# First and fourth attention: second key tile spilled ahead of all stacking, loads requested behind the spills of queries and keys

## The reference, cut to what matters

```python
# x: (16, 112, 256), ctx: (16, 375, 256), 16 heads of 16
qh = heads(layernorm(x) @ W_q.T + b_q)      # layer 3: without biases
kh = heads(ctx @ W_k.T + b_k)
vh = heads(ctx @ W_v.T + b_v)
scores = einsum('bhqd,bhkd->bhqk', qh, kh) / sqrt(16)
attn = softmax(masked(scores), axis=-1)
out = einsum('bhqk,bhkd->bhqd', attn, vh) @ W_o.T (+ b_o)
x = x + out
```

## Time and profile before

| | us |
|---|---|
| median of 3 runs | 2326.16 |
| lowest and highest | 2322.23, 2326.8 |
| the profiled execution | 2323.39 |
| its span, first to last instruction | 2321.6 |
| first attention, about | 26 to 340 |
| fourth attention, about | 1893 to 2222 |

### The profile page before, as it was taken

The page is one execution under the profiler, slowest core; times in us unless marked ns, Lnnn a source line. Parts: engine busy times, 40 slices in busy tenths (PEclk is TensorE's granted clock), DMA queues, the critical chain, the costliest instruction groups (busy, mean ns, idle before and its releaser), DMA issues.

```text
span 2321.6 us, 46633 instructions
## 1 busy us (share of the span) xinstructions
PE 2169.4 (93%) x16038; PEld 1759.9 (76%) x16038; DVE 1285.7 (55%) x3563; ACT 1074.0 (46%) x2929; POOL 448.3 (19%) x478
## 2 busy tenths in 40 slices
PE   7999989999988899999999999999959979988998
PEld 6888877777666667678888788888747758877888
DVE  6877873222244522556556556555542238778766
ACT  5878872222223122244444444444402237877863
POOL 3112201111153345100000000000014421121150
PEclk9999999999999799999999999999969989999999
DMA  8677746222265322110000000001232257767701
GB/s 211 184 193 181 183 116 276 79 86 91 71 178 166 128 66 68 41 46 8 19 27 16 12 14 13 12 8 48 95 113 62 64 143 185 188 175 178 179 19 33
DMA packets 154867, 230.65 MB, mean 99 GB/s; under 512 B 66608, under 2 KB 127488, under 8 KB 152336
## 3 DMA queue, kind: packets, MB, share of 16 engines
q1 hardware_dynamic: 142160, 196.07, 30.4%
q0 software_dynamic: 10656, 29.37, 4.1%
q10 hardware_dynamic: 1824, 2.23, 0.4%
HBM read 176.36 MB, written 51.25 MB: 98 GB/s over the span
## 4 chain that ended last, share of the span: by engine, by line
PE 77%; DVE 7%; DMA 5%; issue 4%; SPq 3%; ACT 2%; POOL 1%; ACTq 0%; DVEq 0%; POOLq 0%
PE bank L2012 9%; PE bank L1157 8%; PE bank L2045 6%; PE bank L1188 6%; PE bank L1043 6%; PE bank L1039 6%; PE bank L2077 5%; PE bank L1083 4%; PE bank L1142 4%; PE bank L1028 3%; PE bank L1135 3%; PE bank L2062 3%; SPq L1523 2%; DMA query_halves<-arena 2%; PE bank L2398 2%
## 5 line engine op out<-in xcount | busy, mean ns | idle before, releaser
L1157 PE MATMUL bank<-ident,arena 112*125 112x112 f32 x2352 | 376.0, 278 | 2.2 <-DVE arena L1395 0.3
L1157 PEld LDWEIGHTS bank<-ident,arena 112*125 112x125 f32 x2352 | 342.8, 191 | 32.2 <-ACT arena L1428 5.8
L1428 ACT ACTIVATE arena<-arena,mx 112x375 f32<-112x375 f32 x512 | 309.3, 605 | 108.6 <-DVE mx L1374 104.5
L1374 DVE CUSTOM_DVE_ANT_0 arena<-bank,maskf 112x375 f32<-112x375 f32 x512 | 272.8, 541 | 101.3 <-PE bank L1135 96.8
L1428 ACT ACTIVATE arena<-bank,mx 112x375 f32<-112x375 f32 x272 | 154.8, 573 | 183.0 <-DVE mx L1386 155.4
L2012 PE MATMUL bank<-arena 128*128 x532 | 231.7, 558 | 2.1 <-ACT arena L2138 2.1
L1135 PE MATMUL bank<-kS,qS 128*112 128x376 f32 x512 | 204.9, 401 | 28.6 <-DMA qS<-query_halves 13.9
L1395 DVE COPY arena<-bank 125x336 f32<-125x336 f32 x448 | 214.1, 501 | 17.3 <-PE bank L1157 17.3
L1188 PE MATMUL bank<-arena 125*32 125x112 f32 (+1 forms) x4608 | 202.6, 265 | 3.1 <-DVE arena L1395 2.9
L1188 PEld LDWEIGHTS bank<-arena 125*32 125x32 f32 (+1 forms) x4608 | 144.3, 118 | 49.8 <-issue 32.5
L1435 ACT ACTIVATE arena<-bank 125x336 f32<-125x336 f32 x336 | 148.3, 442 | 45.4 <-PE bank L1157 44.4
(11 more groups left out here) (266 smaller groups left out, 3699.2 us busy)
## 6 DMA issues: line engine op xcount, KB each, us to landing
kS<-key_halves SPq DMA_DIRECT2D x256, 188.0 KB, 3.9
key_halves<-arena SPq DMA_DIRECT2D x64, 376.0 KB, 4.9
arena<-in_ctxT SPq DMA_DIRECT2D x62, 376.0 KB, 4.9
arena<-in_f_out SPq DMA_DIRECT2D x21, 768.0 KB, 4.5
qS<-query_halves SPq DMA_DIRECT2D x252, 56.0 KB, 2.2
arena<-in_f_up SPq DMA_DIRECT2D x4, 2816.0 KB, 20.0
arena<-results SPq DMA_DIRECT2D x38, 224.0 KB, 5.6
query_halves<-arena SPq DMA_DIRECT2D x32, 224.0 KB, 5.3
```

Source lines behind the costliest of these rows:

```text
L1157: m = pe.transpose(bank[2 + g % 2][0:KT, k * S:(k + 1) * S], pr[:, g % t.NR, k * KT:(k + 1) * KT], ident[0:S, 0:S])
L1374: dve.tensor_tensor_reduce(sm[:, g % 2, :], bank[g % 2][0:S, 0:SK], maskf[:, :], -t.a["scale"], 3e38, ALU.add, ALU.min, mx[:, g % t.NR:g % ...
L1428: act.activation(pr[:, g % t.NR, :], src, ACT.Exp, bias=mx[:, g % t.NR:g % t.NR + 1], scale=-1.0, accum_out=row_sum(t, b)[:, h:h + 1]).the ...
```

## The change

For batches 2 to 15 of both attentions key tile 1 is spilled before any stacking. The loads that stood after batch b now stand, for b of 3 and more, inside batch b+1, behind its spills of queries and key tile 0; for b of 0 to 2 they stay where they were. Those of batch 15, which were none, fall away.

```diff
                 spill_queries()
                 spill_keys(0)
+                if b > LOADS_LATE:
+                    loads(b - 1)
                 if b >= 2:
                     sp.wait_ge(t.scores, t.h0 + (b - 1) * t.H)
+                spill_keys(1)
                 stack_queries()
                 stack_keys(0)
-                spill_keys(1)
                 stack_keys(1)
 
-            for b in range(B):
-                batch(b)
+            LOADS_LATE = 3
+
+            def loads(b):
                 if t.L == 0 and b + 2 < B // 2:
                     rows_of_x(sp, b + 2)
...
                     results_back(sp, t, pair)
+
+            for b in range(B):
+                batch(b)
+                if b < LOADS_LATE:
+                    loads(b)
```

## The result

| | before | changed |
|---|---|---|
| median, us | 2324.19 (4 runs) | 2361.05 (4 runs) |
| lowest and highest | 2317.86, 2326.8 | 2355.98, 2369.08 |
| profiled execution, its span | 2323.39, 2321.6 | 2355.98, 2354.1 |

The ratio is 1.0166, with a 95% interval of 1.0128 to 1.0204: 37 us slower. The forecast was slower by 21 us.

What follows compares the result with a forecast made beforehand. TensorE, busy 2169.4 of 2321.6 us, was almost tied with the spill-and-stack chain. Mean of two counts 18, plus 3 for moved loads, gave +21 us: 2347 us against the timed median 2326.16, range 2325 to 2370.

Steps and rivals of the forecast that it cites:

- The gate (part 1): The first stack waits for VectorE's evacuation of key tile 1, issuing 0.45 us behind it; +22 or +14 us.
- Two of the signs: Expected evidence: SyncE's key-tile waits grow from 27.4 + 23.9 to about 100 us; batches 2 and 3 are already slower.
- The loop count: One batch from head 0 to the next key-0 landing: 20.85 us against 20.3, times 26, +14 us, without clock drops.
- the clock: Rival: after waits near 3 us for stacks TensorE drops to 1.2 GHz; +44 us, 2370 us, chance 0.06.
- The count by batches: Delay less slack over 28 batches: first attention 15.6 us, fourth 6.3 us, sum +22 us.
- the mean of the two counts: Mean of +22 us (delay less slack by batch) and +14 us (batch loop time): 18 us.
- The removed round trip (part 2): SyncE's wait for the key-1 spill's landing, 66.9 + 67.3 us in 28 waits, goes; worth nothing directly.
- The loads (part 3): Moved loads' data stand ahead of the stacks in the DMA queues: 0 to +12 us, taken as 3 us.
- The rival that gave 2319.5 us: Faster case: queueing ahead of the spills matters and positive delays stay hidden; -6.7 us, chance 0.13.
- GpSimd's margin (part 4): Context arrives 2 to 4 us later; GpSimd's 3.9 us margin before VectorE's root covers it; taken at nothing.
- Given back: Rival: heads after a late start run closer, returning over four fifths of the delay; +3 us, 2329 us, chance 0.13.
- The backlog's time, 2360 us: Rival: moved loads' data queue ahead of the stacks at their upper bound; +34 us, 2360 us, chance 0.18.

Runs made afterwards that it cites:

- the last run: Changed kernel with the loads moved behind the key-0 stacks and key tile 1 spilled where it was before: 2390.84 us, ratio 1.028 to the kernel before.

## Why the prediction was right or wrong

**The gate (part 1): right.** The forecast put the first stack 0.45 us behind the evacuation of key tile 1; it is 0.49. The mean delay in the loop is 1.40 us. That the wait is the cause is shown by four runs: the spill alone has the whole loss, an earlier tile takes it away (and does nothing to the kernel before), a later one adds to it, and without the wait (spill between the stacks) the kernel is faster than before. Two of the signs were off. SyncE's waits for key tiles grew from 51 to 148 us and not to about 100, since the waits for tile 0 grew too. And of the batches without moved loads, batch 2 was slower by 1.8 and 0.5 us and batch 3 of the fourth attention by 2.6, but batch 3 of the first took as long as before.

**Its size: too small.** The forecast was +21 us, and it is 32.5 between the profiled executions and 37 between the medians. The loop count gave 20.85 us a batch, or +14; it is 21.46, 0.61 more, which times 26 is 16 us. Of the 0.61, 0.42 lie between head 0 and the next key tile 1: the forecast took 10.15 us, free of clock drops, and it is 10.57. The rest is 0.04 for the gate, 0.07 from the first stack to the landing and 0.08 of slack left. (The 24 batches of the kernel before without a drop have a mean of 10.09 us, so the 10.15 was already a little high.) The mis-sized term is the clock, which the forecast had put with the rivals, with a chance of 0.06. Stretches of the changed kernel, with the granted clock as the last number but two, behind the waits of 1.65 and 2.02 us at 163.9 and 250.7 us:

```profile
165.00:169.00 4.00, 4.00 (x42) 3.47 (x42) 1.79 (x7) 2.33 (x8) 0.00 (x0) 0.65 0.16 54
...
251.00:258.00 7.00, 7.00 (x54) 6.47 (x53) 3.13 (x12) 2.75 (x9) 0.00 (x0) 0.54 0.33 88
```

In batches 2 to 15 of both attentions there are ten such drops to 1.2 GHz, where two were before. Two of them fall into batch 15. Behind each of the other eight the next key tile 1 comes 1.4 to 3.1 us later than in like batches, some 14 us in all, and as that evacuation is the gate, each goes straight into the loop. The forecast was right that the clock falls behind waits, wrong that it takes one near 3 us. The count by batches shows the same: for the first attention it gave 15.6 us, and it is 17.2; for the fourth, where five of the eight drops are, it gave 6.3, and it is 15.1.

The total came as near as it did partly by luck: the 4 us that the mean of the two counts has above the loop count, and the 3 us for backlog, stood where a part of the clock's cost was.

**The removed round trip (part 2): right, worth nothing.** Both waits for landings went, and with the loads alone moved the key-1 wait stayed at 64.9 us in the fastest kernel of all. The rule of the Trainium skill (DMA: Bandwidth & Descriptors, "Rules for kernel authors": issue early, wait late) did overlap the transfer, and these traces show what it cost in the queue: with the transfer its producer's wait was moved ahead of sixteen others.

**The loads (part 3): 3 us forecast, nothing measured.** The forecast said that the query spill would land sooner and nobody would take advantage, and that data ahead of the stacks could cost up to 12 us. The first is so in the changed kernel, and only there. The second isn't: the landing of key-0 stacks takes even 0.13 us less (that the loads drain during SyncE's wait for key tile 1 would explain it, and was not tested). By themselves the loads gain 22 us; added to the moved spill they gain nothing (2361 us with them, 2360 without), since the first stack then waits for the key tile and no longer for the query spill. The rival that gave 2319.5 us for freeing the spills had the mechanism, but tied to the whole change.

**GpSimd's margin (part 4): right.** VectorE's wait for roots is 22.4 us in the changed kernel and 22.3 before, and the last run shows the price beyond the margin.

**Given back: wrong as a rival.** After a late start the next evacuation came no sooner in any batch (9.5 us at the least, as before). The backlog's time, 2360 us, is the median measured, but by another mechanism.

## What to carry to other kernels

In a queue that works in order, an issue that is moved ahead takes its wait for a producer along: before moving it, subtract that producer's end from the start of what would stand behind it, batch by batch, and set the difference against the slack of who waits. Two edits that go in together can have opposite signs and not add up (here +35 and -22 us alone, +37 together): cost and run them apart. Where an engine is tied with a chain of transfers, price short repeated waits not only as idle time but also, with a chance, as a lower clock behind them.

## What the hardware showed beyond that

In the changed kernel waits of 1.6 to 2.4 us at a batch's start were followed by the lower clock in nine batches and not in four others: 1.84 us at 208.0 was not, 1.65 us at 163.9 was. The length of one wait alone doesn't decide it in these traces. What does was not tested.
